# A two-stage kernel (attention, then latent attention with experts): the first weights prepared in two portions, and batch 3 turned into the second output slot

## The reference, cut to what matters

```python
x = x + layernorm(attention(layernorm(x)))   # 16 heads of 64, causal
x = x + layernorm(ffn(layernorm(x)))         # latent attention, then 8 experts

# attention, per batch
q, k, v = (tanh(x @ W + bias) for W, bias in ((Wq, bq), (Wk, bk), (Wv, bv)))
ctx = softmax(mask(q @ k.T / 8)) @ v
out = tanh(ctx @ Wo + bo)

# the experts, on the output o of the latent attention
probs = softmax(o @ router_w + router_b)
w, i = top2(probs); w = w / (w.sum() + 1e-8)
h = gelu(o @ w1[e] + b1[e])
moe = sum over the two chosen e of w_e * (h @ w2[e] + b2[e])
```

## Time and profile before

| | us |
|---|---|
| median of 3 runs | 1686.81 (1686.24 to 1693.86) |
| the profiled execution | 1692.87 |
| its span in the trace | 1690.9 |
| TensorE busy in the span | 1620.2 (96%) |
| VectorE busy | 1437.7 (85%) |
| ScalarE busy | 1207.2 (71%) |
| POOL busy | 456.0 (27%) |

### The profile page before, as it was taken

How to read it: one execution, slowest core, us unless ns; L and a number is a source line. 1 busy time by engine, 2 the same in 40 slices (tenths; PEclk the granted TensorE clock), 3 DMA queues, 4 the chain that set the end, 5 groups by cost and what they waited for, 6 DMA issues and landing times.

```text
span 1690.9 us, 38163 instructions
## 1 busy us (share of the span) xinstructions
PE 1620.2 (96%) x14822; PEld 713.5 (42%) x14822; DVE 1437.7 (85%) x2093; ACT 1207.2 (71%) x1205; POOL 456.0 (27%) x564
## 2 busy tenths in 40 slices
PE   4999999999999999998999999999999999989996
PEld 2444444444444444445233333333332332466774
DVE  6677778888888888897999999999999999478888
ACT  2776666666667666654887888788878888656776
POOL 2311112332322333332234232323332331220004
PEclk9999999999999999998999999999999999989998
DMA  5311101111011001011012000200030000000001
GB/s 153 71 37 38 37 20 39 38 37 37 36 37 37 34 24 38 22 32 32 14 39 49 11 13 16 48 14 13 17 73 22 14 16 14 1 1 14 13 12 50
DMA packets 46754, 53.39 MB, mean 32 GB/s; under 512 B 9309, under 2 KB 33581, under 8 KB 46638
## 3 DMA queue, kind: packets, MB, share of 16 engines
q1 hardware_dynamic: 45588, 50.06, 10.3%
q10 hardware_dynamic: 1050, 1.73, 0.4%
HBM read 15.59 MB, written 10.49 MB: 15 GB/s over the span
## 4 chain that ended last, share of the span: by engine, by line
PE 86%; DVE 6%; ACT 3%; issue 2%; POOL 1%; ACTq 0%; POOLq 0%; DVEq 0%
PE psum L1807 15%; PE psum L567 15%; PE psum L548 11%; PE psum L1792 9%; PE psum L1818 7%; PE psum L512 5%; PE psum L1448 5%; PE psum L1413 4%; PE psum L585 3%; DVE arena L2268 3%; PE psum L605 2%; PE psum L530 1%; ACT arena L2036 1%; PE psum L532 1%; PE psum L531 1%
## 5 line engine op out<-in xcount | busy, mean ns | idle before, releaser
L2268 DVE TENSOR_REDUCE arena<-psum 128x2 f32<-128x1024 f32 x490 | 585.6, 1220 | 39.0 <-PE psum L1818 33.0
L2036 ACT ACTIVATE arena<-psum 128x1024 f32<-128x1024 f32 x512 | 523.8, 1025 | 132.0 <-PE psum L1792 118.0
L721 ACT ACTIVATE arena<-psum 128x2048 f32<-128x2048 f32 (+1 forms) x160 | 274.0, 1712 | 231.6 <-PE psum L548 231.4
L1807 PE MATMUL psum<-arena 128*32 128x256 f32 x4096 | 327.9, 392 | 0.7
L813 POOL TENSOR_SCALAR_AFFINE_SELECT arena<-arena 128x512 f32<-128x512 f32 (+1 forms) x160 | 151.7, 966 | 521.9 <-ACT arena L721 521.9
L567 PE MATMUL psum<-arena,hs 128*64 128x512 f32 (+3 forms) x1536 | 283.0, 496 | 0.1
L548 PE MATMUL psum<-arena 64*128 64x512 f16 (+3 forms) x2304 | 216.3, 325 | 3.8 <-DVE arena L859 3.4
L1792 PE MATMUL psum<-arena 32*128 32x512 bf16 x1024 | 198.9, 385 | 3.7 <-DVE arena L2268 3.1
L1818 PE MATMUL psum<-arena 32*128 32x512 bf16 x980 | 189.1, 382 | 5.9 <-ACT arena L2036 2.4
L859 DVE TENSOR_TENSOR arena<-arena 128x1024 f16<-128x1024 f32 x64 | 80.3, 1255 | 101.0 <-ACT arena L700 101.0
L567 PEld LDWEIGHTS psum<-arena,hs 128*64 128x64 f32 x1536 | 95.9, 136 | 141.4 <-issue 125.2
(11 more groups left out here) (221 smaller groups left out, 2112.7 us busy)
## 6 DMA issues: line engine op xcount, KB each, us to landing
arena<-arena SPq DMA_DIRECT2D x30, 512.0 KB, 2.9
arena<-arena SPq DMA_DIRECT2D x46, 128.0 KB, 2.2
arena<-latent_q SPq DMA_DIRECT2D x64, 64.0 KB, 2.0
arena<-latent_k SPq DMA_DIRECT2D x64, 64.0 KB, 2.0
arena<-arena SPq DMA_DIRECT2D x60, 64.0 KB, 2.4
X<-in_L_attn_states SPq DMA_DIRECT2D x4, 512.0 KB, 6.2
latent_q<-arena SPq DMA_DIRECT2D x16, 96.0 KB, 2.2
latent_k<-arena SPq DMA_DIRECT2D x16, 96.0 KB, 2.3
```

Of the source, the lines that this page charges most:

```text
L721: nc.scalar.activation(probs[g], SC[:, :, 0:WIDTH[g]], ACT.Exp, scale=DH ** -0.5).then_inc(exp_done, 1)
L1807: last = nc.tensor.matmul(OT[ROWS * c:ROWS * (c + 1), h * HALF // 2:(h + 1) * HALF // 2], v_cols[par][:, kt, 2 * pr + i, :], e_probs[u % 4 ...
L2036: nc.scalar.activation(e_probs[u % 4], src, ACT.Exp, scale=KD ** -0.5).then_inc(e_done, 1)
L2268: nc.vector.tensor_reduce(half_tops[:, kh, qt, 2 * pr:2 * pr + 2], src.rearrange("p (i c) -> p i c", i=2), AX.X, ALU.max).then_inc(top_don ...
```

## The change

In words:

- Block 1 loads Wk's rows on SP's queue, and no DMA spreads Wk[0] any more; all three first rows are loaded by ACT's queue, ahead of Wv and Wq, and spread by TensorE.
- Each weight is prepared in two portions: pairs 0 and 1 (256 of 1024 columns), and pairs 2 to 7. Block 1 prepares the first portion whole and subtracts the first row for two of the second ones; the rest stands at the head of block 2. SP's loads for pair 2 and VectorE's first sums wait for it (`w_rest`).
- In block 2 TensorE begins with `project(0, 0)` and `project(0, 1)`, the second into `OUT`; `values(0)` and the turning of the biases follow.
- The moments, deviations and norms of batches 2 and 3 are moved into pairs 0 and 1, those of batch 1 behind `low_part(0, 1)`.
- In the passage batch 3 is turned into `YP[1]`, and its logits go there too. TensorE does `output(0)` before `route_last`. VectorE does `add(0, 0)` before `take_last_logits`, and the routing weights of batch 3 only after `add(0, 2)`. `turn_weights` stands behind the hidden layers of unit 4, the biases one unit later, and experts 2 and 3 are written out of TensorE's loop.

The diff, cut to its core:

```diff
-        SPREAD = {2: bank(2, 2), 0: bank(4, 2)}
+        SPREAD = {2: bank(2, 2), 0: bank(4, 2), 1: bank(6, 2)}
+        SLOTS = ((2, VSLOT), (0, QSLOT), (1, KSLOT))
+        EARLY_PAIRS = (slice(0, 2), slice(2, PAIRS))
...
+        def less_first(dve, part, k):
+            t = SLOTS[k][0]
+            if part == 0:
+                dve.wait_ge(w_got[t], 16 * 3)
+                dve.wait_ge(first_spread, k + 1)
+            v = pair_weights(part, k)
+            first = SPREAD[t].rearrange("p (n c) -> p n c", n=PAIRS)[:, EARLY_PAIRS[part], :]
+            nc.vector.tensor_tensor(v, v, first, ALU.subtract).then_inc(w_less, 1)
+        def weights_hi(act, part, k):
+            act.wait_ge(w_less, 3 * part + k + 1)
...
+        def weights_lo(dve, part, k):
+            dve.wait_ge(whi_done, 3 * part + k + 1)
...
                 load_states(0)
-                for t, w in ((2, Wv), (0, Wq)):
-                    sp.dma_start(first_rows[0:1, t, :], w[0:1, :]).then_inc(rows_got, 16)
-                for rows in REST:
-                    sp.dma_start(w_first[rows, 1, :], Wk[0, :].partition_broadcast(rows.stop - rows.start)
...
+                for rows in REST:
+                    sp.dma_start(w_in[rows, 1, :], Wk[rows, :]).then_inc(w_got[1], 16)
...
                 for t, w in ((2, Wv), (0, Wq), (1, Wk)):
+                    act.dma_start(first_rows[0:1, t, :], w[0:1, :]).then_inc(rows_got, 16)
+                for t, w in ((2, Wv), (0, Wq)):
...
                 state_moments(dve, 0)
-                less_first(0)
+                less_first(dve, 0, 0)
+                less_first(dve, 0, 1)
+                weights_lo(dve, 0, 0)
                 dve.wait_ge(consts, 2)
                 norm_states(dve, 0)
-                less_first(1)
-                less_first(2)
-                for k in range(3):
-                    weights_lo(k)
+                less_first(dve, 0, 2)
+                weights_lo(dve, 0, 1)
+                less_first(dve, 1, 0)
+                weights_lo(dve, 0, 2)
+                less_first(dve, 1, 1)
                 states_lo(dve, 0, bank(0, 2))
...
             def pair(i, par, last=False, norm=False):
+                if not at_least(i, 1):
+                    sp.wait_ge(w_rest, 3)
...
-            values(0, 0)
             project(0, 0, 0)
             project(0, 1, 0)
+            values(0, 0)
+            turn_biases()
             scores(0, 0, 0)
...
+            weights_hi(act, 1, 0)
+            weights_hi(act, 1, 1)
             tanh(0, 0, 0)
             tanh(0, 1, 0)
+            value_tanh(0, 0)
+            weights_hi(act, 1, 2)
+            take_biases()
...
                 mask(i, 0)
                 if not at_least(i, 1):
                     split_wo()
+                if not at_least(i, 2):
+                    state_deviation(pool, 2 + i)
...
                 mask(i, 3)
...
-            for b in range(1, B):
-                state_deviation(pool, b)
+            state_deviation(pool, 1)
...
                 if norm:
                     tile_moments(t)
+                if not at_least(i, 2):
+                    state_moments(dve, 2 + i)
                 hi_second(i, par, 0)
                 hi_second(i, par, 1)
+                if not at_least(i, 1):
+                    norm_states(dve, 2)
...
                     invert(i - 1)
+                    if not at_least(i, 2):
+                        norm_states(dve, 3)
...
-            for b in range(1, B):
-                state_moments(dve, b)
-            dve.wait_ge(consts, 6)
+            less_first(dve, 1, 2)
+            weights_lo(dve, 1, 0)
+            weights_lo(dve, 1, 1)
+            low_part(0, 0, 0)
+            low_part(0, 1, 0)
+            state_moments(dve, 1)
+            weights_lo(dve, 1, 2)
             norm_states(dve, 1)
-            low_part(0, 0, 0)
-            norm_states(dve, 2)
-            low_part(0, 1, 0)
-            norm_states(dve, 3)
...
-        BIASES_AT = 2
+        BIASES_AT = 3
...
             def turn_last():
                 pe.wait_ge(proj_added, 2 * B)
-                pe.wait_ge(lg_ready, 2 * EARLY)
+                pe.wait_ge(raw_copied, 2 * N2)
                 for t in range(T):
-                    last = nc.tensor.transpose(TURNED[:, t * P:(t + 1) * P], acc[:, EARLY * T + t, :], ident[:, :])
+                    last = nc.tensor.transpose(YP[1][:, t * P:(t + 1) * P], acc[:, EARLY * T + t, :], ident[:, :])
...
                 if isinstance(n, int) and n == 0:
-                    pe.wait_ge(mT_ready, 2 * B)
-                    pe.wait_ge(mhi_ready, 2 * B)
+                    pe.wait_ge(lg_ready, 2 * EARLY)
                 elif isinstance(n, int) and n == 1:
-                    pe.wait_ge(raw_copied, 2 * N2)
                     pe.wait_ge(lg_ready, 2 * EARLY + 1)
...
             def expert(e, par, biases=False):
                 for b in range(B):
                     hidden(e, par, b)
+                    if biases and b == 0:
+                        turn_weights()
                     output(B * e + b - 1, par if b > 0 else 1 - par, (b - 1) % 2)
-                    if biases and b < B - 1:
-                        bias(b + 1)
+                    if biases:
+                        bias(b)
...
             hidden_half(0, 0, 2, 0)
+            output(0, 0, 0)
             route_last()
-            output(0, 0, 0)
             hidden_half(0, 0, 2, 1)
             output(1, 0, 1)
             hidden(0, 0, 3)
-            turn_weights()
             output(2, 0, 0)
-            bias(0)
             expert(1, 1, biases=True)
-            with pe.Fori(1, E // 2) as k:
+            for par in range(2):
+                expert(2 + par, par)
+            with pe.Fori(2, E // 2) as k:
...
             finish_weights(0)
+            add(0, 0)
             take_last_logits()
             centre(1)
-            add(0, 0)
-            softmax(1)
-            find_largest(1)
-            finish_weights(1)
             for e in range(2):
                 for b in range(1 if e == 0 else 0, B):
+                    if e == 0 and b == EARLY:
+                        softmax(1)
+                        find_largest(1)
+                        finish_weights(1)
```

More of the change, by code:

```diff
@@ L504, in project @@
                 x_now, _, w_now = weights(n, par)
-                if j == 0:
+                dst = PJ
+                if isinstance(n, int) and n == 0:
+                    if j == 1:
+                        pe.wait_ge(w_less, 6)
+                        dst = OUT
+                elif j == 0:
                     pe.wait_ge(vals_ready, n + 1)
@@ L525, in values @@
                 elif n > 0:
-                    pe.wait_ge(tanh_done, 4 * n)
+                    pe.wait_ge(vals_ready, n)
+                else:
+                    pe.wait_ge(tanh_done, 2)
                 for t in range(T):
@@ L740, in pair @@
                     copy_out(i - 1, 1 - par)
+                else:
+                    begin_acc(0)
                 if last:
@@ L766, in pair @@
                     take_states(2 + i)
+                if isinstance(i, int) and i == 1:
+                    order_latent_weights()
             def first_states():
@@ L902, in lo_first @@
                 dve.wait_ge(masked, 3 * i + 1)
+                if not at_least(i, 1):
+                    dve.wait_ge(w_rest, 3)
                 if at_least(i, 2):
@@ L1539, in third_scalar @@
             unit(0, 2)
+            unit(0, 3)
             exponentials(act, 1)
-            unit(0, 3)
+            unit(1, 0)
             act.wait_ge(cT_ps, 1)
             nc.scalar.copy(cT, HP[0][:, 0:2 * P]).then_inc(cT_ready, 1)
-            for b in range(B):
+            for b in range(1, B):
                 unit(1, b)
```

103 lines of the change are left out of this document (50 added, 53 removed).

## The result

The changed kernel takes 1704.83 us, median of 5 runs (1704.65 to 1707.66); the kernel before took 1686.81 (1686.17 to 1693.86) beside it. The ratio is 1.0091, interval 1.0068 to 1.0113. That is 18 us slower, outside the range of 1682 to 1697, and beyond the +8.4 us to which the prediction gave a chance of 0.08.

A forecast was written before the change was run, and what follows sets the result against it. TensorE, busy 96% of the span, was taken as the bound, with time to win where it waits or runs at low clock. Start -2.3 and passage +5.3 gave +3.0 us on 1686.81: 1690 us, range 1682 to 1697.

The forecast's parts named there:

- Block 1 and the first scores: Start: block 2 begins at 23.8 us, 1.5 gained; scores(0,0) start at 32.7 and end 8.8 us earlier.
- the dropped bytes: Block 1: 508 KB less DMA spreading of Wk[0], worth 2.1 us by the skill's rule; 1.5 was taken.
- What is given back: Pairs 0 and 1: moved moments, deviations and norms cost 3.1 and 2.8 us, plus 0.6 in pair 2; sum 6.5.
- part 1: Block 1, head of block 2 and steps moved into pairs 0 and 1: -8.8 + 6.5 = -2.3 us.
- shared time of POOL and VectorE: Start: 0.6 us added, counted only in the slower bound of +1.2 us.
- rival A: Pairs 0 and 1: low clock strikes there too, 3 to 6 us more, total 1693 to 1696; chance 0.16.
- output(1) starts at 1499.9 after 5.9 us: Passage: output(1) waits 5.9 us for batch 3's logits behind finish_weights(0) and add(0,0), starting at 1499.9 against 1498.50.
- part 2: Passage into the experts: new order costs +3.5 and one bias +1.8, together +5.3 us.
- turn_weights' wait: Passage: turn_weights stands behind about 6 us of idle TensorE, with batch 3's weights there at 1519.0.
- the low clock at outputs 1 and 3: Passage: both run at the low clock behind waits, 5.2 and 5.1 us; at full clock both 2.5 shorter.
- one bias more: Passage: one more bias is left to do behind hidden(5), 1.8 us.
- On the median 1689.8: Whole kernel: +3.0 us, 1695.9 in the profiled execution's terms, carried to the median 1686.81 as 1689.8, said as 1690.

The follow-up runs named there:

- pool_late: Changed kernel with POOL's low_act of unit 2 waiting until add(0,0) is done; 1702.69 us, ratio 1.0071 to the kernel before.
- early_index: Changed kernel with the 24 index searches of finish_weights(0) moved into an idle stretch of VectorE; 1705.61 us, ratio 1.0096 to the kernel before.
- index_pool_apart: Changed kernel with index searches moved early and GpSimd's low(3) and low_act(2) put behind finish_weights(0); 1699.82 us, ratio 1.0052 to the kernel before.
- passage_only: Kernel before with only the change's new passage to the experts, its start left as it was; 1699.03 us, ratio 1.0063 to the kernel before.
- mask_first: Changed kernel with state_deviation(2 + i) behind mask(i, 3) on POOL instead of ahead of it; 1702.15 us, ratio 1.0078 to the kernel before.
- before_shift: Kernel before with 12 idle matmuls of 128 columns on TensorE ahead of scores(0,0); 1692.05 us, ratio 1.0016 to the kernel before.

## Why the prediction was wrong

- **Block 1 and the first scores: right.** 23.77 for 23.8, 32.14 for 32.7, scores in 1.48 us. By the rule of the Trainium skill (DMA: Bandwidth & Descriptors, "Issuing engines are not separate DMA queues") the dropped bytes would have given 2.1 us, and the trace has 1.5; the 8.98-us issue both began earlier and got shorter, so the rule is not settled by this.
- **"What is given back", 6.5 us: the failed step of part 1.** The first scores ended 9.2 us early (33.6 for 42.8) and pair 3 began 3.4 late, so 12.6 were given back. 7.2 of them went in pair 0 (forecast 3.1), 5.0 in pair 1 (2.8) and 0.4 in pair 2 (0.6). The places were right (POOL's masks of pairs 0 and 1, then turn_normal), the durations were not. I took the norm at 2.1 and the deviation at 2.0 us from rows at the head of block 2, where POOL did nothing but deviations and VectorE moments and norms; in the pairs each norm took 2.87, each deviation 3.8 (1.13 and 2.60), and the norm of batch 1 in front of them 3.96. The "shared time of POOL and VectorE", which I had priced at 0.6 and only for the end of a range, is the missing term, with rival A's. Start: +3.4 where -2.3 was forecast.
- **Rival A: it was there.** The 5.23 and 3.34 us of waiting each brought a context at 3.5 for 1.94 us, with the clock at 0.50, so 1.6 twice. That is 3.2 together, the low end of its 3 to 6; it came on top of the rest.
- **"output(1) starts at 1499.9 after 5.9 us": the failed step of part 2.** I took finish_weights(0) at its old length. In the old order POOL's low_act(2) came after it; the new one puts it beside it. +3.7 us, as pool_late and the pair early_index and index_pool_apart show. Everything else of the passage came as reckoned: turn_weights' wait, the low clock at outputs 1 and 3 (4.62 and 5.33 us), one bias more. +8.3 for +5.3; the lacking 3 us are this one.
- **The leg between the stages had no term.** The forecast took it as unchanged without saying so; it was 2.4 us longer, and in medians possibly more.
- **"On the median 1689.8": a step that carried too much.** I moved a difference between two executions to the medians as it was. The profiled executions differ by 13.9 us, the medians by 18, since the profile of before was 6.1 above its median and that of after 2.0 above its own. In the old order of the passage four profiles show 69.16 to 71.85 us, in the new one five show 80.07 to 80.57: the old one has better runs than the one I reckoned from, the new one shows none. Between the stages the leg was 727.81 and 730.25 in the two profiles, and 723.65 in passage_only's, so there too one execution stands for little. Together the misses are 5.7 us at the start, 3.0 in the passage, 2.4 on the leg and 4.1 from profile to median, the 15 us between 1689.8 and 1704.83.

## What to carry to other kernels

Before moving a step to another place in a queue, look at what the other of VectorE and GpSimd does there: a step of 0.2 us costs what is left of its neighbour's, and the row of a step in a quiet stretch is no price for a busy one. When the named releaser is taken away and nothing moves, as in mask_first, read what TensorE waits for next; there it was the chain through VectorE. Where the clock falls in some runs only, compare medians of many runs of both kernels, and do not carry a difference of two executions over to the medians.

## What the runs showed of the hardware

- VectorE's f32 steps with two inputs in SBUF end with GpSimd's running f32 `tensor_tensor`, or a step's own length behind it: 0.20, 0.36 and 0.36 us became 2.07, 1.87 and 2.25. Its copy of 128x48 indices to f32 took 0.71 to 2.03 and ended with GpSimd's step each time. Reciprocal (0.30), index search (0.16) and, in index_pool_apart, eight adds with one input from PSUM (2.16) kept their lengths beside it.
- Which step stands beside which decides. The norm (2.11) kept its length beside GpSimd's power of 128x8 and took 2.87 to 3.96 beside its masks and scaling. Beside GpSimd's `tensor_scalar` of 128x1024 (L834 of the kernel before, to 48.87) VectorE's L907 took 1.79 for 0.95 and ended at 47.93, ahead of it, so there the rule of the first point is not exact.
- The index searches thus hid 3.4 us of GpSimd's work; moved away, they gained nothing.
- The scores behind a wait of 3.4 us took 2.74 us in three traces of the old start, and 1.48 in before_shift, which fills that wait with idle matmuls. The projection ahead of the filler was fast too there, so the cause is not shown.
- Between the stages the granted clock stood at 0.50 in some executions and at 1.00 in others with the same code there, with legs from 723.65 to 731.21 us. With 14 idle matmuls in the gap ahead of it the runs of the kernel before lay closer (highest 1691.45 for 1697.54), but its trace still has 0.50 there.
